# Experts of a mixture layer: first-layer products over four PSUM banks, a pair of experts on the two partition halves

## The reference, cut to what matters

```
xn = layernorm of a token's 64 features; xe = xn * ln_g[e] + ln_b[e]
h = gelu(xe @ W1[e] + b1[e])          # 8 experts, 64 -> 256
y = h @ W2[e] + b2[e]                 # 256 -> 64
out = sum over the top 2 experts of weight * y
```

## Time and profile before

| | |
|---|---|
| median of 3 runs | 400.85 us (400.56 to 401.72) |
| profiled execution, its own time | 402.59 us |
| its span, first to last instruction | 400.9 us |
| mean granted TensorE clock | 0.944 of full speed |
| busy: PE, DVE, ACT, POOL | 337.8, 330.0, 280.1, 265.9 us |

### The profile page before, as it was taken

One profiled execution on the slowest core, in us unless ns is written; L12 is line 12 of the kernel. 1 busy time (PEld: TensorE's weight loads), 2 busy tenths in 40 slices (PEclk: granted clock), 3 DMA queues, 4 the chain that ended last, 5 costly groups with the idle time before them and its releaser, 6 DMA issues. The chain is left out here.

```text
span 400.9 us, 5477 instructions
## 1 busy us (share of the span) xinstructions
PE 337.8 (84%) x1658; PEld 183.1 (46%) x1658; DVE 330.0 (82%) x454; ACT 280.1 (70%) x458; POOL 265.9 (66%) x270
## 2 busy tenths in 40 slices
PE   0597896677899889989998898899889877999794
PEld 0484445333455345444544453455245425555452
DVE  2774457997899999999999999999999988994411
ACT  1002667488968997898799869987987757761472
POOL 8706112986579966994899589858985994692122
PEclk9996999588999999998999999999989986999899
DMA  8771079899899698659975897589758960000000
GB/s 196 211 146 19 0 191 222 214 222 227 206 229 217 149 213 205 155 147 212 206 165 133 199 234 164 137 191 222 166 150 194 222 141 1 2 0 15 1 0 13
DMA packets 21236, 59.52 MB, mean 148 GB/s; under 512 B 4924, under 2 KB 13272, under 8 KB 15320
## 3 DMA queue, kind: packets, MB, share of 16 engines
q1 hardware_dynamic: 20040, 58.34, 63.4%
q10 hardware_dynamic: 1168, 0.84, 0.9%
HBM read 53.93 MB, written 5.24 MB: 148 GB/s over the span
## 5 line engine op out<-in xcount | busy, mean ns | idle before, releaser
L347 POOL TENSOR_TENSOR hs<-hs,Cs 128x1024 f32<-128x1024 f32 x63 | 149.3, 2373 | 42.8 <-DVE hs L769 42.2
L769 DVE TENSOR_TENSOR_SCAN hs<-av,P 128x1024 f32<-128x1024 f32 x64 | 146.3, 2286 | 4.7 <-PE P L1056 1.3
L635 ACT ACTIVATE hb<-P,b1c 128x512 f32<-128x512 f32 x128 | 81.5, 683 | 18.6 <-PE P L1179 16.3
L762 DVE SCALAR_TENSOR_TENSOR P<-P,bbcol,ub 128x1024 f32<-128x1024 f32 x62 | 79.7, 1285 | 2.4 <-DMA ub<-u_scratch 1.1
L1192 PE MATMUL P<-hb,W2s 128*64 128x256 f32 x512 | 69.3, 394 | 0.0
L1178 PE MATMUL P<-X,W1H 128*128 128x512 f32 x128 | 60.1, 469 | 5.6 <-ACT hb L635 4.4
L1179 PE MATMUL P<-X,W1L 128*128 128x512 f32 x128 | 52.6, 411 | 0.0
L578 ACT ACTIVATE av<-P,Aneg 128x510 f32<-128x510 f32 x68 | 44.1, 686 | 10.9 <-PE P L1131 6.9
L359 POOL TENSOR_TENSOR accs<-accs,mes 128x256 f32<-128x256 f32 x56 | 40.9, 730 | 14.1 <-DVE mes L860 9.5
L1192 PEld LDWEIGHTS P<-hb,W2s 128*64 128x64 f32 x512 | 31.6, 137 | 31.0 <-issue 21.1
L860 DVE SCALAR_TENSOR_TENSOR mes<-P,cols,wbs 128x256 f32<-128x256 f32 x64 | 27.3, 467 | 16.9 <-PE P L1192 9.6
(11 more groups left out here) (191 smaller groups left out, 478.8 us busy)
## 6 DMA issues: line engine op xcount, KB each, us to landing
ub<-u_scratch SPq DMA_DIRECT2D x31, 1024.0 KB, 10.8
av<-dt_scratch SPq DMA_DIRECT2D x15, 1024.0 KB, 7.4
dt_scratch<-dts SPq DMA_DIRECT2D x7, 256.0 KB, 2.8
u_scratch<-rl SPq DMA_DIRECT2D x7, 256.0 KB, 2.8
av<-in_L_conv_Wr SPq DMA_DIRECT2D x2, 576.0 KB, 6.9
av<-in_L_conv_Wl SPq DMA_DIRECT2D x2, 576.0 KB, 7.7
res<-in_x SPq DMA_DIRECT2D x4, 256.0 KB, 4.5
hb<-in_L_ffn_W SPq DMA_DIRECT2D x2, 512.0 KB, 6.4
```

The costliest lines, as they stand in the source:

```text
L347: gp.tensor_tensor(hs[:, at, :, :], hs[:, at, :, :], rep(Cs[:, p, :], 1, 2), ALU.mult).then_inc(S["cm"], 1)
L635: a_.activation(hb[:, r % 4, :], P[:, (XA, XB)[r % 2], :], ACT.Gelu, bias=b1c[:, r:r + 1]).then_inc(S["gl"], 1)
L762: v.scalar_tensor_tensor(out=ring, in0=rep(P[:, BB, :], 1, 2), scalar=bbcol[:, 0:1], in1=ub[:, 2 * n:2 * n + 2, :], op0=ALU.add, op1=ALU.m ...
L769: v.tensor_tensor_scan(hs[:, (SLOTS * g + n) % RING].rearrange("p a t -> p (a t)"), av[:, 2 * n:2 * n + 2, :].rearrange("p a t -> p (a t)" ...
```

## The change

It has two parts that are tied together.

- First layer: steps 0 to 3 go into four different banks (XB, YS, XD, XA), so that none of them waits for a gelu. Steps 4 to 7 follow one at a time between the second-layer steps. The two warm-up products ahead of the stage are gone. The weights' transposes and spreads use YS, and the copy of the step sizes on ScalarE (act_dhi) moves from the first to the seventh pair of gelus.
- Second layer: pe_f2 is one product of 512 columns. Even experts write partitions 0 to 63, odd ones 64 to 127, of a whole bank. dve_expert handles a pair at once with 512 columns, four instead of eight per group. GpSimd adds three times 512 columns instead of eight times 256. TensorE folds the halves with a 128 x 64 matrix of two identities (pe_fold) one group later. ScalarE copies the fold out, and GpSimd adds it to t1, which is written out from there. VectorE's products move one slot forward (after slots 3, 4, 5 and 6 instead of 4, 5, 6 and 7). In the tail the last fold goes to YS, and VectorE adds it.

```
-                dve_slot(eng, i, 4)
-                experts(0)
+                experts(0)
+                dve_slot(eng, i, 4)
+                experts(1)
                 dve_slot(eng, i, 5)
+                experts(2)
...
                 dve_slot(eng, i, 6)
-                experts(4)
+                experts(3)
                 dve_slot(eng, i, 7)
...
-                experts(6)
```

```
+        def f1_bank(r):
+            return (XB, YS, XD, XA, XB, XD)[r] if r < 6 else (XA, XB)[r % 2]
...
         def pe_f1(eng, g, r):
...
-            if r >= 2:
-                eng.wait_ge(S["gl"], EXP * KC * g + r - 1)
-            bank = (XA, XB)[r % 2]
+            if r >= 4:
+                eng.wait_ge(S["gl"], done + (1, 3, 4, 5)[r - 4] if r < 8 else done + r - 1)
+            bank = f1_bank(r)
...
         def pe_f2(eng, g, r):
             e, k = r // KC, r % KC
             eng.wait_ge(S["gl"], EXP * KC * g + r + 1)
             pair = r // (2 * KC)
             if r == 0:
-                eng.wait_ge(S["e2"], g + 1)
+                eng.wait_ge(S["o2"], g + 1)
+                since(eng, "ev", g)
...
-            for h in range(2):
-                last = pe.matmul(P[64 * h:64 * h + 64, (XC, XD)[pair % 2], HW * (e % 2):HW * (e % 2) + HW], W2s[:, e, k, :],
-                                 hb[:, r % 4, HW * h:HW * h + HW], start=(k == 0), stop=(k == KC - 1))
-            last.then_inc(S["f2"], 1)
+            at = 64 * (e % 2)
+            pe.matmul(P[at:at + 64, (XC, XD)[pair % 2], :], W2s[:, e, k, :], hb[:, r % 4, :],
+                      start=(k == 0), stop=(k == KC - 1)).then_inc(S["f2"], 1)
...
+        def pe_experts(eng, g):
+            for r in range(4):
+                pe_f1(eng, g, r)
+            if g > 0:
+                pe_fold(eng, g - 1)
+            pe_f1(eng, g, 4)
+            pe_f2(eng, g, 0)
+            pe_wt(eng, g)
+            pe_f2(eng, g, 1)
+            pe_f1(eng, g, 5)
+            pe_f2(eng, g, 2)
+            pe_f1(eng, g, 6)
+            pe_wb(eng, g, 0)
+            pe_f2(eng, g, 3)
+            pe_f1(eng, g, 7)
+            pe_f2(eng, g, 4)
+            pe_f2(eng, g, 5)
+            pe_wb(eng, g, 1)
+            for n in range(4, 8):
+                pe_pair(eng, g, n)
+                if n < 6:
+                    pe_wb(eng, g, n - 2)
...
+        def pe_fold(eng, g):
+            eng.wait_ge(S["acc"], 3 * g + 3)
+            eng.wait_ge(S["o2"], g + 2)
+            for h in range(2):
+                last = pe.matmul(P[64 * h:64 * h + 64, XC, HW:T], foldm[:, :], acc[:, HW * h:HW * h + HW], start=True, stop=True)
+            last.then_inc(S["fold"], 1)
```

More of the change, by code:

```diff
@@ L61 @@
 lg lgb m1 dd ex s1 ms1 o1 e2 m2 s2 s2r ms2 o2 den rden num wt wn vhi vlo wtr wtc wb_mm wb
-f1 gl f2 me acc out_sem""".split()
+f1 gl f2 me acc fold ev fin k_fold out_sem""".split()
 def rep(ap, axis, n):
@@ L259, in sp_spread @@
             for c in range(CHUNKS):
+                if c == 1 and g >= 3:
+                    sp_out(sp_, g - 3, (g - 3) % 2)
                 since(sp_, "scan", SLOTS * (g - 1) + 2 * c + 2)
@@ L301, in _ @@
             row("b_dt", b_dt.unsqueeze(0))
+            for k in range(2):
+                sp_.dma_start(rows[R["b2"]:R["b2"] + PAIRS, 64 * k:64 * k + 64], b2.rearrange("(j k) d -> k j d", k=2)[k]).then_inc(S["ld_rows"], 16)
             sp_.dma_start(bbc[:, :], b_bc.rearrange("(a s) -> a s", a=2)).then_inc(S["ld_rows"], 16)
             for h in range(2):
-                for name, ap in (("b_out", b_out.unsqueeze(0)), ("b2", b2), ("cb2", cb2.unsqueeze(0)), ("ln_g", ln_g), ("ln_b", ln_b)):
+                for name, ap in (("b_out", b_out.unsqueeze(0)), ("cb2", cb2.unsqueeze(0)), ("ln_g", ln_g), ("ln_b", ln_b)):
                     n = ap.shape[0]
@@ L315, in _ @@
             sp_.dma_start(brs[:, :], rep(fbr, 0, 128)).then_inc(S["ld_dup"], 16)
-            for g in range(2):
+            for g in range(G):
                 sp_spread(sp_, g, g % 2)
[L318 to L322, removed]
+            for g in range(G - 3, G):
+                sp_out(sp_, g, g % 2)
             sp_.wait_ge(S["out_sem"], 32 * G)
@@ L466, in body, with weighted @@
                 q = 1 - p
-                def weighted(lo):
+                def weighted(j):
                     if prev is not None:
-                        for e in range(lo, lo + 2):
-                            pool_acc(eng, prev, q, e)
+                        pool_acc(eng, prev, j)
                 if i == 0:
@@ L510, in _ @@
             pool_router(eng, G - 1)
-            for e in range(EXP):
-                pool_acc(eng, G - 1, 1, e)
+            pool_out(eng, G - 2)
+            for j in (1, 2):
+                pool_acc(eng, G - 1, j)
         def act_lnA1(eng, g, bank=XD):
@@ L695, in body @@
                             act_wb(eng, prev, n - 2)
+                        if n == 6 and nxt is not None:
+                            act_dhi(eng, nxt)
                 if nxt2 is not None:
@@ L1042, in _ @@
             dve_router2(eng, G - 1)
-            for e in range(EXP):
-                dve_expert(eng, G - 1, e)
+            for j in range(PAIRS):
+                dve_expert(eng, G - 1, j)
+            eng.wait_ge(S["fold"], G)
+            eng.wait_ge(S["fin"], G - 1)
+            v.tensor_tensor(t1[:, (G - 1) % 2, :], P[:, YS, 0:HW], t1[:, (G - 1) % 2, :], ALU.add).then_inc(S["fin"], 1)
         def pe_sum(eng, g, k):
@@ L1052, in pe_sum @@
                 eng.wait_ge(S["aexp"], NBLK * g + 15)
-                since(eng, "wb", EXP // 2 * min(g, G - 1))
+                since(eng, "wb", PAIRS * min(g, G - 1))
             for q in range(4):
@@ L1106, in pe_po @@
             eng.wait_ge(S["yg"], g + 1)
-            since(eng, "me", EXP * g)
+            since(eng, "me", PAIRS * g)
             eng.wait_ge(S["sg"], so_far(g, 3))
@@ L1153, in pe_wt @@
             eng.wait_ge(S["vlo"], g + 1)
[L1154 to L1157, removed]
+            eng.wait_ge(S["gl"], EXP * KC * g + 2)
+            for h in range(2):
+                for q in range(2):
+                    at = HW * h + 128 * q
+                    pe.transpose(P[0:2 * EXP, YS, at:at + 128], vv[:, q, h].rearrange("p r e -> p (r e)"), ident[:, :]).then_inc(S["wtr"], 1)
         def pe_wb(eng, g, r):
@@ L1344, in body @@
                     eng.wait_ge(S["xn1"], so_far(prev, 3))
-                    since(eng, "me", EXP * prev)
+                    since(eng, "me", PAIRS * prev)
                     pe_warm(eng, 2, XD)
```

164 lines of the change are left out of this document (85 added, 79 removed).

## The result

The changed kernel takes 467.03 us (median of 4 runs, 466.21 to 467.94), against 400.71 before (4 runs). The ratio is 1.165, with a 95% interval of 1.162 to 1.169: slower by 66 us. It lies inside the stated range (434 to 470) and 14 us above the predicted 453. Two single runs further down were far slower than the others of their kernel, 612.57 us (first part alone) and 538.37 us (tail alone): they count in the medians given there, but not in the ratios.

A forecast was written before the change was run, and what follows sets the result against it. Two chains of nearly equal length, VectorE's own work and TensorE's stage, were taken to bound the kernel. Bodies and tail added 51.6 us to 402.6, giving 454.2; less 1.7 for the median, about 452.5, stated as 453, range 434 to 470.

The forecast's parts named there:

- The second-layer products: TensorE's second-layer steps no longer run side by side: 0.925 us a step against 0.51, 6.7 us more per group.
- The head of the stage: Start of TensorE's experts' stage: with four banks the first second-layer step starts at 224.3, not 225.20.
- From there to the end of pair 8: TensorE from first second-layer step to pair 8's end: 24.95 us, so pair 8 ends 5.5 us later.
- From there to the gate: Pair 8's end to VectorE's gate: last expert product, slot 7, slot 0 and gate take 8.1 us, where it was 6.4.
- The rival of the falling clock: TensorE's new 2.1 us gap before pe_b halves its clock: 11.5 us more over six bodies, 464; chance 0.25.
- Tail: After the last body: last second-layer step ends at 399.9, not 395.65; 3.9 us more after savings on additions.
- The sum: Whole kernel: bodies 1 to 5 add 36.0, body 6 5.7, body 7 6.0, tail 3.9; in all 51.6 us.
- the likeliest case: Whole kernel: the main forecast of 453 us, with 449 to 457 and a chance of 0.45.
- The waits did not give way: Rival in the bodies: gaps take back 1.7 us and up to 1.4 more; 434 to 442; chance 0.15.
- The full factor of two: Rival on second-layer steps: a lone step costs the 1.02 us of a former pair; 464; chance 0.08.

The follow-up runs named there:

- first part alone: Kernel before, with only the first-layer part: four banks, new order of steps 0 to 7, no warm-up products; 400.9 us, ratio 0.999.
- tail alone: Kernel before, with four banks and single first-layer steps at the stage's head in the tail only; 400.37 us, ratio 1.001.

## Why the prediction was right, and where 14 us were missing

- **The second-layer products.** The step that carried the prediction holds. I put a step at 0.925 us in place of 0.51; two measure 1.86. The reading that line 1192's products ran side by side is now shown, since the order alone halves their time. One thing here was wrong: I wrote that the queue never puts steps of different halves next to each other. In bodies 6 and 7 and in the tail it does, and four steps that I had put at 3.7 us took 2.24.
- **The head of the stage.** The first second-layer step was to start 12.9 us after the gate (224.3 less 211.39), and it started 13.03 after it. The fold (247.52) and its copy (0.39 us) lie where I placed them.
- **From there to the end of pair 8** I had 24.95 us. It was 25.86 (249.02 to 274.88). Two terms were too small and make up 0.8 of the missing 0.91: the spread of a pair's weights at 0.30, which is 0.42 (four times), and a step that stands alone, 1.00 (252.23 to 253.23) and not 0.925 (four times). I take the change to the narrow form and back for the reason; no run shows it by itself. Bodies 1 to 5 were thus 4.6 us short.
- **From there to the gate** I had 8.1 us, with slot 7 queued behind the last product. That the two are chained was right: putting the product back gave 17.2 us. With the clock kept up it is 8.04 us and a body 46.9, the 45.9 forecast and 0.91 missing as above. Without it, it was 9.45 in the body shown (274.88 to 284.33).
- **The rival of the falling clock** had a chance of 0.25 and came true besides the forecast, not in place of it. Its mechanism was as described (the wait of 2.1 us, line 1121 at half speed), and its size was off: not 11.5 us in six bodies but 1.4 us in each of bodies 3 to 5 (and in body 6 an amount that no run separates), and filling the wait gave back 4.5. The other falls, at the heads of bodies 5 and 7 (1.5 and 1.9 us more to the first second-layer step), were in no rival.
- **Tail:** 3.9 us forecast, 4.1 measured, and that is luck. The first second-layer step started 12.19 us after the gate (435.94 less 423.75) and not 11.5. The stage behind it was some 0.6 us shorter than the 23.05 forecast: 1.5 less by the neighbours on different halves, 0.9 more by the undersized terms. The two errors cancel.
- **The sum.** Seven bodies were to bring 47.7 us (36.0 + 5.7 + 6.0) and brought 59.0. Bodies 1 to 5 miss 9.9 of the 11.3: 4.6 are the undersized terms, 5.7 the clock in bodies 3 to 5, and body 1 was 0.6 shorter than these would make it. Bodies 6 and 7 miss the other 1.4 although their stages were shorter than forecast; the clock was at half behind the wait of body 6 and at the head of body 7. The remaining 3 of the 14 us are in neither bodies nor tail: they come from how far each profiled execution was from its median, and from time outside the span. My own range for the likeliest case, 449 to 457, took in one of these prices (the step) and neither of the two that moved; it was too narrow.
- **The other rivals.** The waits did not give way: in bodies 1 to 5 every one of VectorE's four expert products waited, 1.65 to 3.01 us each. The full factor of two (1.02 us a step) is out by 1.86 for two, though a lone step costs 1.00.

## What to carry to other kernels

The products with 64 output columns here left half of TensorE to a neighbour in the queue on the other partition half. A layout in which neighbours share a half took a step from 0.51 to 0.93 us without adding a multiplication, so look at the order in the queue before the count of instructions. And an instruction that waits for a late producer should stand behind everything on its engine that someone else needs: here 0.75 us of work in the wrong place cost 17 us.

## What the runs showed of the hardware that I had not expected

- Narrow products need not alternate to run side by side. Four instructions on partitions 0 to 63 followed by four on 64 to 127 took 1.87 us, the time of one half's four alone (1.86).
- Equal waits of TensorE were not followed by the same clock. Behind the wait of 2.14 us in the changed kernel it stayed full in bodies 1 and 2 and was at 0.50 within 1.5 us in bodies 3 to 5. A wait of 0.63 us at 294 us was followed by 0.50 as well. In the kernel before, the wait of 1.28 us was not followed by a fall and the one of 1.47 us at 376 us was. So the length of one wait does not tell what the clock will do.
- One profiled execution can make a fall of the clock look like the effect of a change: here 1.45 us in the tail of the kernel before.
